# Last batch's value sums from split operands in a fused attention and mixture-of-experts kernel

## The reference

```python
xn = layernorm(x)                                     # per token
q, k = xn @ w_q, xn @ w_k                             # 64 columns each
scores = where(causal, q @ k.T * 64 ** -0.5, -inf)    # per batch, 1024 x 1024
values = (xn @ w_v1) @ w_v2                           # 128 -> 64 -> 128
attention = softmax(scores) @ values
shared = silu(xn @ w_gate.T) * (xn @ w_up.T) @ w_down.T
experts = sum over the top 1 of 16 experts: (up * silu(gate)) @ down_proj
out = x + attention + shared + experts
```

## Time and profile before

| | us |
|---|---|
| median of 3 runs | 218.97 (218.88 to 220.79) |
| profiled execution | 219.1 |
| its span, first to last instruction | 217.3 |
| busy PE / DVE / ACT / POOL | 202.7 / 148.7 / 126.5 / 140.3 |
| mean granted TensorE clock | 0.992 |

### The profile page before, as it was taken

The page is one execution under the profiler, slowest core; times in us unless marked ns, Lnnn a source line. Parts: engine busy times, 40 slices in busy tenths (PEclk is TensorE's granted clock), DMA queues, the critical chain, the costliest instruction groups (busy, mean ns, idle before and its releaser), DMA issues.

```text
span 217.3 us, 4526 instructions
## 1 busy us (share of the span) xinstructions
PE 202.7 (93%) x1288; PEld 162.7 (75%) x1289; DVE 148.7 (68%) x352; ACT 126.5 (58%) x295; POOL 140.3 (65%) x244
## 2 busy tenths in 40 slices
PE   4899979799999999994999999999999999999994
PEld 4688857588878866552879999999998986675673
DVE  2997696867778795991276786666666665958632
ACT  2368356467659788665345545554444687876651
POOL 3477790088888888884009989898988877072000
PEclk9999999999999999999799999999999999999999
DMA  5999999711128115514622322233326400494051
GB/s 155 287 336 338 297 289 436 311 35 43 37 51 217 38 51 123 152 44 76 38 47 81 87 80 78 64 89 92 89 84 178 113 9 0 126 326 130 0 149 48
DMA packets 30262, 28.37 MB, mean 131 GB/s; under 512 B 8835, under 2 KB 26378, under 8 KB 29600
## 3 DMA queue, kind: packets, MB, share of 16 engines
q1 hardware_dynamic: 27712, 23.85, 38.7%
q0 software_dynamic: 2528, 4.24, 6.1%
HBM read 14.36 MB, written 10.50 MB: 114 GB/s over the span
## 4 chain that ended last, share of the span: by engine, by line
PE 55%; POOL 28%; DVE 7%; issue 5%; DMA 3%; ACT 0%; DVEq 0%; POOLq 0%; SPq 0%
POOL scratch L451 16%; PE acc L1509 10%; POOL wel L425 6%; PE big L1189 5%; PE big L1187 5%; PE big L1188 5%; PE mid L1498 5%; PE mid L1378 5%; PE acc L1395 5%; POOL rows L435 4%; PE acc L1419 3%; POOL rstd L386 3%; PE mid L1337 2%; PE big L1362 2%; PE big L1359 2%
## 5 line engine op out<-in xcount | busy, mean ns | idle before, releaser
L477 POOL DMA_INDIRECT y_rows<-y,slot_info x47 | 47.2, 1005 | 22.9 <-ACT y L1130 14.3
L451 POOL DMA_INDIRECT scratch<-rows,slot x32 | 35.2, 1100 | 15.7 <-DVE slot L702 10.5
L766 DVE TENSOR_REDUCE negmax<-big 128x1 f32<-128x128 f32 (+7 forms) x32 | 23.9, 752 | 11.3 <-PE big L1362 10.9
L1068 ACT COPY pt<-mid 128x512 f32<-128x512 f32 (+3 forms) x48 | 21.9, 483 | 16.0 <-PE mid L1378 14.4
L856 DVE COPY eht<-mid 128x512 f32<-128x512 f32 (+1 forms) x24 | 16.3, 679 | 19.4 <-PE mid L1498 19.4
L1130 ACT COPY y<-acc 128x256 f32<-128x256 f32 (+1 forms) x24 | 8.8, 368 | 31.3 <-PE acc L1509 30.2
L1509 PEld LDWEIGHTS acc<-wed,eht 128*128 128x128 f32 x188 | 24.4, 191 | 2.0 <-issue 0.4
L1054 ACT ACTIVATE prob<-big,negmax 128x128 f32<-128x128 f32 (+7 forms) x32 | 23.8, 747 | 2.8 <-DVE negmax L766 2.6
L1509 PE MATMUL acc<-wed,eht 128*128 x188 | 24.9, 275 | 0.0
L863 DVE SCALAR_TENSOR_TENSOR eh<-esg,slot_info,big 128x256 f32<-128x256 f32 x47 | 20.5, 477 | 5.3 <-ACT esg L1120 4.9
L1378 PE MATMUL mid<-identf,prob 128*128 128x128 f32 x144 | 22.8, 282 | 0.2 <-ACT prob L1054 0.2
(11 more groups left out here) (144 smaller groups left out, 459.2 us busy)
## 6 DMA issues: line engine op xcount, KB each, us to landing
we_raw<-w_gate_up SPq DMA_DIRECT2D x4, 1024.0 KB, 10.8
scratch<-blank SPq DMA_DIRECT2D x1, 3120.0 KB, 16.7
xe<-scratch SPq DMA_DIRECT2D x24, 130.0 KB, 2.2
q_raw<-qk_all SPq DMA_DIRECT2D x8, 256.0 KB, 5.0
k_raw<-qk_all SPq DMA_DIRECT2D x8, 256.0 KB, 5.0
wed<-w_down SPq DMA_DIRECT2D x1, 2048.0 KB, 16.9
expert_out<-y_rows SPq DMA_DIRECT2D x8, 256.0 KB, 4.4
out<-res SPq DMA_DIRECT2D x7, 256.0 KB, 3.0
```

Source lines behind the costliest of these rows:

```text
L451: pool.indirect_dma_start(scratch, bass.IndirectOffsetOnAxis(ap=slot[:, t:t + 1], axis=0), rows[:, t, :], None).then_inc(row_sent[t % FLY] ...
L477: pool.indirect_dma_start(y_rows, bass.IndirectOffsetOnAxis(ap=slot_info[:, t, 0:1].bitcast(U32), axis=0), y[p % NY][:, t % 2, :], None, b ...
L766: dve.tensor_reduce(negmax[:, i:i + 1], buf[:, at:at + (i + 1) * P], AX.X, ALU.max, negate=True).then_inc(max_ready, 1)
```

## The change

The last batch only. GpSimd, behind its last indirect write, splits the values into a high part (rounded to fp32r) and a low part (the rest), side by side in `v_hl`, 128 columns per key tile. ScalarE writes `pt` of the last batch as fp32r (`pth`), and VectorE writes the rest, bank minus `pth`, as a second fp32r part (`ptl`, `pt_lo`). `weigh_last` now serves both groups: two fp32r products per step, `v_hl` with `pth` and with `ptl`, into all 128 rows of `acc[g]`, over all columns of the step. The left and right sides are gone: both `keep_last` copies wait for all of `pv_done`, and `outputs(3, 0)` uses 128 rows for its first tile too. Transposes of steps 6, 7, 10 and 11 of the last batch go to the two banks of `big[0]`, so that four banks are in turn (`pt_bank`), and from step 2 on they wait for the subtraction that read their bank (`ptl_ready`). GpSimd adds returned groups 0 to 5 in place of 0 to 3, VectorE 6 and 7, the first of them earlier than before.

```diff
+        v, _ = overlay(wel_start, [("v_hl", [P, BT, P], F32R)] + [(f"ptl{n}", [P, GC], F32R) for n in range(PTS)])
...
-        right = big[1][:, GC:2 * GC]
...
+        def pt_bank(b, n):
+
+            if b == B - 1 and n >= GT and n % PTS >= 2:
+                return big[0][:, n % PTS % 2 * GC:(n % PTS % 2 + 1) * GC]
+            return mid[n % 2]
...
+            v_last = vr_all[:, (B - 1) * BT:B * BT, 0:KD]
+            pool.tensor_copy(v_hl[:, :, 0:KD], v_last).then_inc(v_hi_ready, 1)
+            pool.wait_ge(v_hi_ready, 1)
+            pool.tensor_tensor(v_hl[:, :, KD:P], v_last, v_hl[:, :, 0:KD].bitcast(F32), ALU.subtract
+                               ).then_inc(v_lo_ready, 1)
             for g in range(ON_POOL):
...
+            def pt_lo(*steps):
+
+                for n in steps:
+                    _, c0 = block_of(n)
+                    dve.wait_ge(pt_ready, FIRST + (B - 1) * STEPS + n + 1)
+                    if n >= PTS:
+                        dve.wait_ge(pv_done, FIRST + (B - 1) * STEPS + n + 1 - PTS)
+                    dve.tensor_tensor(ptl[n % PTS][:, c0:GC], pt_bank(B - 1, n)[:, c0:GC],
+                                      pth[n % PTS][:, c0:GC].bitcast(F32), ALU.subtract).then_inc(ptl_ready, 1)
...
             sums(2)
             row_max(3, 1, 2)
             split_q_lo(3, 1)
-            row_max(3, 3, 4, 5)
+            row_max(3, 3)
+            add_returned(DVE_ORDER[0])
+            row_max(3, 4, 5)
             add_attention(2, 0)
             row_max(3, 6, 7)
+            pt_lo(0, 1)
             keep_mixed(2, 1)
-            add_returned(DVE_ORDER[0])
+            pt_lo(2, 3)
+            add_returned(DVE_ORDER[1])
             add_attention(2, 1)
-            add_returned(DVE_ORDER[1])
+            pt_lo(4)
             sums(3)
-            add_returned(DVE_ORDER[2])
-            add_returned(DVE_ORDER[3])
+            pt_lo(5, 6, 7)
             add_attention(3, 0)
+            pt_lo(8, 9, 10, 11)
             add_last(0)
...
-                    act.copy(pt[n % PTS][:, c0:GC], mid[n % 2][:, c0:GC]).then_inc(pt_ready, 1)
+                    kept = pth if b == B - 1 else pt
+                    act.copy(kept[n % PTS][:, c0:GC], pt_bank(b, n)[:, c0:GC]).then_inc(pt_ready, 1)
...
             def keep_last(part):
-
-                if part == 0:
-                    act.wait_ge(left_done, 1)
-                else:
-                    act.wait_ge(pv_done, FIRST + B * STEPS)
+                act.wait_ge(pv_done, FIRST + B * STEPS)
                 cols = slice(part * GC // 2, (part + 1) * GC // 2)
-                act.copy(mixed[1][:, cols], (right if part else acc[1])[:, cols]).then_inc(last_kept, 1)
+                act.copy(mixed[1][:, cols], acc[1][:, cols]).then_inc(last_kept, 1)
...
+                    if b == B - 1 and n >= 2:
+                        pe.wait_ge(ptl_ready, n - 3 if n >= 2 * GT else min(n, GT + 1) - 1)
...
+            def weigh_last(*steps):
...
+                    pe.wait_ge(pt_ready, FIRST + (B - 1) * STEPS + n + 1)
+                    pe.matmul(dst, v_hl[:, kb, :], pth[n % PTS][:, c0:GC], start=kb == 0, stop=False,
+                              skip_group_check=True)
+                    pe.wait_ge(ptl_ready, n + 1)
+                    pe.matmul(dst, v_hl[:, kb, :], ptl[n % PTS][:, c0:GC], start=False, stop=True,
+                              skip_group_check=True).then_inc(pv_done, 1)
...
-                keys = KD if g == 0 and r == 0 else P
+                keys = KD if b < B - 1 and g == 0 and r == 0 else P
...
-            weigh(3, 0, 1)
+            weigh_last(0, 1)
...
-ON_POOL = 4
+ON_POOL = 6
-DVE_ORDER = (6, 7, 4, 5)
+DVE_ORDER = (6, 7)
```

More of the change, by code:

```diff
@@ L96, in build @@
         we_raw = nc.alloc_sbuf_tensor_at("we_raw", [P, NE, 2 * FE], F32, offset=top[0])
+        wel_start = top[0]
         wel = sb("wel", [P, NE, 2 * FE], F32R)
@@ L154, in build @@
         prob, pt, mixed = [c[PROB_ORDER.index(i)] for i in range(BT)], c[BT:BT + PTS], c[BT + PTS:]
+        pth, _ = overlay(att_start + sum(size([P, (i + 1) * P], F32) for i in PROB_ORDER),
+                         [(f"pth{n}", [P, GC], F32R) for n in range(PTS)])
+        v, _ = overlay(wel_start, [("v_hl", [P, BT, P], F32R)] + [(f"ptl{n}", [P, GC], F32R) for n in range(PTS)])
+        v_hl, ptl = v[0], v[1:]
         (rt_over,), b_end = overlay(c_end, [("rt_over", [1, NS, NE], F32)])
@@ L187, in build @@
         mixed_kept, mixed_out = sem("mixed_kept", 2), sem("mixed_out", 2)
-        last_kept, last_out, left_done = sem("last_kept"), sem("last_out"), sem("left_done")
+        last_kept, last_out = sem("last_kept"), sem("last_out")
+        v_hi_ready, v_lo_ready, ptl_ready = sem("v_hi_ready"), sem("v_lo_ready"), sem("ptl_ready")
         ln_step, var_ready, rstd_ready = sem("ln_step"), sem("var_ready"), sem("rstd_ready")
@@ L356, in _ @@
                 sp.wait_ge(y_summed, g + 1)
-                store(g * GT)
-            for g in DVE_ORDER[BG:]:
-                sp.wait_ge(last_summed, DVE_ORDER.index(g) + 1)
                 store(g * GT)
@@ L1375, in transposes @@
                         pe.wait_ge(eht_ready, NP)
+                    if b == B - 1 and n >= 2:
+                        pe.wait_ge(ptl_ready, n - 3 if n >= 2 * GT else min(n, GT + 1) - 1)
                     for r in range(c0 // P, GT):
                         pe.wait_ge(exp_done, FIRST + b * BT + g * GT + r + 1)
-                        last = pe.transpose(mid[n % 2][:, r * P:(r + 1) * P],
+                        last = pe.transpose(pt_bank(b, n)[:, r * P:(r + 1) * P],
                                             prob[g * GT + r][:, kb * P:(kb + 1) * P], identf[:, :])
@@ L1397, in weigh @@
                               ).then_inc(pv_done, 1)
-            def weigh_last(side, *steps):
+            def weigh_last(*steps):
                 for n in steps:
                     kb, c0 = block_of(n)
-                    if kb == 0 and side == 0:
-                        pe.wait_ge(att_added[1], FIRST + B - 1)
-                    pe.wait_ge(pt_ready, FIRST + (B - 1) * STEPS + n + 1)
-                    half = kb % 2 * KD
-                    first, stop = (c0, GC // 2) if side == 0 else (max(c0, GC // 2), GC)
-                    dst = acc[1][half:half + KD, first:stop] if side == 0 else right[half:half + KD, first:stop]
-                    last = pe.matmul(dst, flat(vr_all[:, (B - 1) * BT + kb:(B - 1) * BT + kb + 1, 0:KD]),
-                                     pt[n % PTS][:, first:stop], start=kb < 2, stop=True, skip_group_check=True)
-                    if side:
-                        last.then_inc(pv_done, 1)
-                    elif n == 2 * GT + 1:
-                        last.then_inc(left_done, 1)
+                    g = 0 if n < GT else 1
+                    dst = acc[g][:, c0:GC]
+                    if kb == 0:
+                        pe.wait_ge(att_added[g], FIRST + B - 1)
+                    if n == 0:
+                        pe.wait_ge(v_lo_ready, 1)
+                    pe.wait_ge(pt_ready, FIRST + (B - 1) * STEPS + n + 1)
+                    pe.matmul(dst, v_hl[:, kb, :], pth[n % PTS][:, c0:GC], start=kb == 0, stop=False,
[3 more added lines that the diff above has]
+                              skip_group_check=True).then_inc(pv_done, 1)
             def to_output(b, g, r):
-                keys = KD if g == 0 and r == 0 else P
+                keys = KD if b < B - 1 and g == 0 and r == 0 else P
                 return pe.matmul(weighed(b, g, r), mixed[g][0:keys, r * P:(r + 1) * P], wv2[0:keys, :], start=True,
@@ L1591, in _ @@
             transposes(3, 3, 4)
-            weigh(3, 2, 3)
+            weigh_last(2, 3)
             transposes(3, 5)
@@ L1595, in _ @@
             transposes(3, 6, 7)
-            weigh_last(0, 4, 5)
-            weigh_last(1, 4, 5)
+            weigh_last(4, 5)
             transposes(3, 8, 9)
-            weigh_last(0, 6, 7)
-            weigh_last(1, 6, 7)
+            weigh_last(6, 7)
             transposes(3, 10, 11)
-            weigh_last(0, 8, 9)
-            weigh_last(1, 8, 9, 10, 11)
+            weigh_last(8, 9, 10, 11)
             last_output(0)
```

## The result

| | kernel before | changed kernel |
|---|---|---|
| median, us | 220.38 | 221.62 |
| lowest to highest, us | 217.25 to 225.42 (16 runs) | 219.68 to 222.78 (16 runs) |
| ratio | | 1.0103 [1.0061, 1.0145] |
| profiled execution, us | 219.1 | 221.32 |
| its span, us | 217.3 | 219.5 |

The kernel became slower, by 1.03% in this ratio and by 0.56% in the medians, where the prediction had 0.2% and a range up to 220.8 us. The ratio is the mean of the 16 changed runs over the mean of the 11 fast runs of the kernel before (217.25 to 220.48 us), its five runs from 220.74 us on being left out as slow, while the means of all sixteen against all sixteen give 1.0052. The median of the kernel before is itself 1.4 us above the three runs shown ahead; both have to be explained.

What follows compares the result with a forecast made beforehand. It took TensorE's own work near the end, then the serial copy, output product, addition and store, as the bound. Terms -0.15 - 0.30 + 0.35 + 0.30 + 0.25 = +0.45 on 218.97 gave 219.4 us, range 218.0 to 220.8.

Steps and rivals of the forecast that it cites:

- Value sums: Last batch on TensorE: two fp32r products per step take 4.94 us against 5.10 before, 0.15 us less.
- output product: Output products of group (3,0): first tile uses 128 keys instead of 64, 0.30 us less; bounds 0 and 0.46.
- VectorE's waits: TensorE waits on VectorE's new queue: `outputs(2, 1)` about 0.2 us, late low parts; 0.30 us more, bounds 0.1 and 1.2.
- Rival 4: Value sums: an fp32 step had cost twice two fp32r products, so 4.1 us gained, 215.0 us; chance 0.02.
- Rival 2: VectorE becomes the bound through longer subtractions or late handovers: 0.9 us more, 220.3 us; chance 0.10.
- Rival 1: No changeover cost, wait for low parts or held cast: 1.05 us less than forecast, 218.35 us; chance 0.22.
- GpSimd's split: GpSimd's value split holds VectorE's key cast at 186.59 us, delaying TensorE: 0.25 us more; bounds 0 and 1.45.
- Rival 3: GpSimd excludes every VectorE instruction: at both places 2.4 us more, 221.8 us; one alone 220.6; chance 0.08.
- Last copy and output: Serial end after the last product: both copies now wait for it, 2.03 us against 1.68, 0.35 us more; bounds 0.2 and 0.5.
- Sum: All terms together: +0.45 us on the median of 218.97 us, giving 219.4 us, called no change.
- The range: Whole kernel: 218.0 to 220.8 us; chance 0.90 within 1%, 0.04 faster and 0.06 slower by over 1%.
- What would show it: Signs in the trace; the forecast is wrong if the last product ends before 212.6 or after 213.8 us.

Runs made afterwards that it cites:

- e6: Changed kernel with VectorE's four additions of group (3,0) moved behind its last four subtractions; 221.23 us, ratio 1.0060 to the kernel before.
- e3: Changed kernel with GpSimd's value split moved behind its fourth addition of returned rows; 220.85 us, ratio 1.0038 to the kernel before.
- e4: Kernel before with only GpSimd's value split added, its result unused; 220.77 us, ratio 1.0012 to the kernel before.
- e1: Kernel before, run again unchanged; 220.31 us, ratio 1.0003.
- e11: Changed kernel, split behind fourth addition, (3,0) additions behind last subtractions, steps 10 and 11 in their own bank; 220.93 us, ratio 1.0010 to the kernel before.
- e2: Changed kernel, run again unchanged; 222.21 us, ratio 1.0103 to the kernel before.
- e10: Changed kernel, split behind fourth addition, (3,0) additions behind last subtractions, group (3,1) in two sides; 220.69 us, ratio 0.9981 to the kernel before.
- e5: Changed kernel with group (3,1) summed in two sides again, with split operands; 221.72 us, ratio 1.0062 to the kernel before.
- e8: Changed kernel: split late, two sides, (3,0) additions behind subtractions, transposes of steps 6 and 7 first; 221.16 us, ratio 1.0028 to the kernel before.
- e9: Changed kernel with value split behind fourth addition and (3,0) additions behind last subtractions; 220.82 us, ratio 1.0000 to the kernel before.

## Why the prediction was wrong, step by step

- **Value sums, -0.15, output product, -0.30, and VectorE's waits, +0.30: the sum held, the terms did not.** They made -0.15, and B moved by -0.11. A pair of fp32r products costs what was taken: steps 4 and 5 are 0.93 us (210.28 to 211.21), 0.92 was taken. The output products of (2,1), whose copy stands behind two subtractions, cost 0.20 more, the 0.2 that was named. But the value products with their own waits came to +0.35, where -0.15 and the remaining 0.1 make -0.05: steps 0 and 8 wait for their low parts (0.48 and 0.50 on the chain for 0.23 to 0.31). The output products of (3,0) take 1.16, 0.19 less and not 0.30. What made up for it is a term that the prediction left out: transposes behind value products take 0.46 less. It had charged the change from transposes to fp32r products, five times 0.1, and put nothing for the change back. That B came out nearly right is luck in good part.
- **Rival 4**, a step in fp32 at twice two fp32r products, is refuted by B. The Trainium skill's four passes (FP8 and Floating Point Precision, TensorE Precision Notes) may well be true of one product; in this kernel two fp32 steps of 64 columns take 1.01 us together, hardly more than the 0.93 of the four fp32r products in their place.
- **Rival 2**, VectorE as the bound at +0.9, did not come: subtractions of 512 columns take 0.64 to 0.68 us, and e6 took only 0.24 out by order. Rival 1, none of the small costs, did not come either: e3 and e4 measure the held cast, e6 a wait for a low part.
- **GpSimd's split, +0.25: right mechanism, wrong size.** It costs 0.33 to 0.59 us, 0.59 in the profile after. The term was worked out from the distance of 185.0 to 186.59 in one trace; for that distance the rule under e4 gives 0.26, as forecast. But the distance floats: it is 1.60 in the profile ahead, 1.33 in e1, the same kernel, 1.28 in the changed kernel and 1.83 in e11, though none of their code up to there differs but for the split. The mechanism was the one stated: the Trainium skill (SBUF — State Buffer, Who interferes with whom) exempts VectorE instructions with one SBUF input outside the two-port modes, and the trace agrees: four additions beside GpSimd's split 1.13 us, subtractions of `ptl` at 208.75 and 209.46 beside GpSimd's addition at 208.91, 0.68 and 0.64.
- **Rival 3, that GpSimd holds every VectorE instruction: refuted** by the same rows. The change came out slower, but not in the way, nor at the place, that this rival named.
- **Last copy and output, +0.35: too small.** C is 2.21, +0.53. The two output products behind the pause take 0.50 on the chain, not 0.39: that row was of a product with others ahead of it. The handoff to VectorE is 0.12 (0.03, 0.05 and 0.04), where 0.04 was taken. The bound of 0.5 was nearly right, the value in it not.
- **Sum.** The terms gave +0.45, the stages measured +1.01: 0.34 from the split, 0.18 from the end, 0.04 from B. On the base that the prediction took, 218.97 us, this is 219.98 and inside its range.
- **The range: the step that failed most.** It was laid around 218.97, a median of three runs, as if it were the kernel's. Runs at a mean clock of 0.99 lie at 218.9 us and those at 0.974 at 221.5, and 79 of 105 runs of the kernel before are of the two lower bands; its median here is 220.4. With +1.0 that makes 221.4, close to the 221.62 measured. Nothing in the working asked how much the clock could move a run; the page had the stretch at half clock, and I did not price it, and one of the three runs, 220.79, already stood apart. The ratio would be about 1.0046 by the stages (1.01 of 219). The medians give 1.0056, and the step from there to 1.0103 lies mostly in the five longest runs of the kernel before, which that ratio leaves out. What is left I put down to the mix of bands, by the argument under e1 and e2, and it stays an inference.
- **What would show it.** The last product ended at 214.85, outside 212.6 to 213.8. Less the 1.2 of clock alone it is at 213.65, inside. A criterion on absolute times mixes what a change does with what came before it; distances between two events of one trace would have said at once which term failed.

No version that keeps the low part is measurably faster than the kernel before. The best ratio of these, e10's 0.9981 [0.9941, 1.0021], cannot be told from 1, and its stages are 0.28 us over.

## What to carry to other kernels

Before costing a change from one profile, look how far its granted clock and its median are from typical, and compare stages between events of one trace, not absolute times: a ratio of 1% here was half change, and half which executions were compared. Work moved to an idle engine has a price where it shares a port with the chain: place it where the other engine's two-port instructions are not due, and price it by its end, not by its start. And splitting operands pays only against what the old products cost where they stand: here two fp32 products in the two halves of the output rows cost 1.01 us together, 0.51 for a step of 512 columns, and the two fp32r products of a step cost 0.47. A stage that comes out as forecast is no proof of its terms: look at each of them.

## What the runs showed of the hardware that was not expected

- A stretch at 1.2 GHz after an idle of some 3 us is 3.4 us long in one execution of the kernel before and 6.8 in another; it is 10.2 in the profiled run of e5. Two bands are 1.0 to 1.7 us apart. Why an execution gets one or the other, no run here shows.
- A VectorE cast of 512 columns, 0.42 us by itself, took 0.75 to 1.00 beside a GpSimd subtraction, always ending a little after it, while GpSimd's subtraction kept its 1.28. With two SBUF inputs either side can be the longer one: in the earlier trace rows both were stretched, while in e4 a subtraction of `k_lo` took 1.50 us for 0.68 and GpSimd's addition beside it kept its 1.27.
- An output product behind a pause has its result after 0.50 us (215.29 in the changed kernel), one with others ahead of it after 0.39.
- With the last two pairs of stores 0.5 us apart, the end of the span came 2.95 to 2.97 us behind the last addition (e8, e10), with 0.96 us between them 2.54 to 2.55 (e6, e9).
